# Causal mask of an attention's max pass: added by VectorE in the instruction that takes the maximum, in place of mask matmuls on TensorE

## The chip, the cores and the metric

The kernel runs on one core of a Trainium2 chip. The metric is the time on the device for one execution, in microseconds (us); lower is better. The engines are TensorE (PE in the rows, its weight loads PEld), VectorE (DVE), ScalarE (ACT), GpSimd (POOL) and SyncE (SP), which here only issues DMAs (SPq in the rows).

## The reference, cut to what matters

Two layers, each a mixer and a feed-forward with modulation, over x of 16 batches, 512 tokens, 256 channels. The change touches the mixer of the second layer, a causal attention with 16 heads of 16 channels:

```python
q, k, v = (x @ w_qkv).reshape(B, T, 3, H, HD) ...          # B 16, T 512, H 16, HD 16
scores = einsum('bhqd,bhkd->bhqk', q, k) * SCALE
scores = where(causal, scores, -inf)                        # key after query: never
scores = scores + head_scales * q_proj[..., :, None] * k_proj[..., None, :]
attn = softmax(scores, axis=-1)
out = einsum('bhqk,bhkd->bhqd', attn, v) ... @ w_out
```

The added rank-one term is folded into the q weights, so that one product gives the scores. Softmax subtracts the maximum of each row (each query) over the keys that it may see.

## The kernel before, in words

Ahead of the attention are the first layer and the modulation; behind it are a router and experts. All of these are left as they are. The attention takes 16 batches (NB) one after the other, and in each 16 heads.

**Two passes over the scores.** q and k are written as three bf16 parts each, stored to `qk_parts` in DRAM and loaded again into `q_stack` and `k_stack`, 96 rows of partitions per head (`sp_store`, `sp_load`). The *max pass* computes scores with queries on the partitions (`pe_max`), and VectorE takes the maximum of each row (`dve_max`) into `top`. TensorE turns `top`, VectorE splits it into three bf16 parts (`dve_neg_max`), and SyncE copies these into three more rows of `q_stack` (`sp_row`). The *second pass* computes the scores again, with keys on the partitions and the maximum subtracted by the product itself (`pe_scores`), ScalarE takes the exponential (`act_exp`), and TensorE multiplies it with the values, four heads at a time (`pe_pv`).

**Tiles and banks of the max pass.** A head has four query tiles of 128 rows. Tile qt sees (qt + 1) x 128 keys, so the widths are 512, 384, 128 and 256. They come as three *fills* of a PSUM bank: tile 3; tiles 2 and 0 side by side; tile 1. Two banks are used in turn, fill n (three per head) in bank MAX0 + n % 2. TensorE may write fill n when VectorE has read fill n - 2 (semaphore `mxr`), and VectorE may read it when TensorE's last matmul of the fill is done (`mxp`).

**The mask before.** The last 128 columns of each tile hold the diagonal block. Behind each score matmul, a second one of ident_b with mask_q (128 x 128, bf16, zero or -3.0e38 where key > query) adds the mask to those columns (L1194). The second pass does the same with mask_k (L1212).

**Order of the work.** Each engine's list is written out by hand, one function per engine and batch (`pe_batch`, `dve_batch`, `act_batch`, `sp_batch`), and goes in order. In TensorE's list, at head h and fill f of batch i, the second pass of head h comes first and then the max pass of head h + 7 (AHEAD), which from h = 9 on is a head of batch i + 1. Seven heads of the max pass run ahead of the first batch. Other work stands between the heads: the values at h = 0, the turning of the normed x at 1, the q and k projections of the next batch at 3 and 4, the turning of `top` at 1, 5, 9 and 13, the products with the values at the third fill of 0, 4, 8 and 12, and the output projection of the batch before at 7 and 8. SyncE's list in a batch is: row copy of group 1, stores of q and k parts of the next batch, row copy 2, loads of the next batch's groups 0 and 1 (a group is four heads), row copy 3, load 2, row copy 0 of the next batch, load 3.

The lines of the profile that matter: L1192 score matmul of the max pass, L1194 its mask matmul, L1210 and L1212 the same of the second pass, L1414 the maximum, L1430 to L1437 `dve_neg_max`, L1457 rest of q and k parts, L1544 the exponential, L1638 the third q and k parts on GpSimd, L1659 the stores, L1671 the loads, L1677 the row copies. L2047 and L1469 are VectorE instructions elsewhere that the prediction compares with.

Of the kernel before, what the change touches and what calls it, by code (L numbers as in the profile page):

```python
# [27 lines left out]
P = 128  # L28
# [993 lines left out]
         (1, (0, 3), slice(0, 3)), (1, (3, 5), slice(0, 2)), (1, (5, 6), slice(0, 1)))  # L1022
N_STORES = 2 * 3 * 2
STACK = len(Q_PARTS) * HD


def attention_weights(nc, t, ps, mem, wq, wk, wv, wo, ident_b, mask_q, mask_k):


    with ExitStack() as ctx:  # L1030
        def sb(name, shape, dt=F32):
            return ctx.enter_context(nc.sbuf_tensor("aw_" + name, shape, dt))

        def sem(name):
            return ctx.enter_context(nc.semaphore("aw_" + name))

        f_qT, f_q = sb("qT", [P, DK, D]), sb("q", [P, DK, D])
        f_k, f_v, f_o = sb("k", [P, DK, D]), sb("v", [P, DK, D]), sb("o", [P, DK, D])
        dirs, sdirs, scales = sb("dirs", [HEADS, D]), sb("sdirs", [HEADS, D]), sb("scales", [HEADS, 1])
        form = sb("form", [P, DK, D])  # L1040
        masks = sb("masks", [P, 2, P])
        small, big, fold, prod, hi, lo, const = (sem(n) for n in ("small", "big", "fold", "prod", "hi", "lo", "const"))
        block = ctx.enter_context(nc.Block())

        @block.sync
        def _(sp):
            sp.dma_start(dirs[:, :], t["head_dirs"]).then_inc(small, 16)
            sp.dma_start(scales[:, :], t["head_scales"]).then_inc(small, 16)
            sp.dma_start(f_qT[:, :, :], t["wqT"].rearrange("(k p) n -> p k n", p=P)).then_inc(small, 16)
            for n, f in enumerate((f_k, f_v)):  # L1050
                sp.dma_start(f[:, :, :], t["w_qkv"][:, (n + 1) * D:(n + 2) * D].rearrange(
                    "(k p) n -> p k n", p=P)).then_inc(big, 16)
            sp.dma_start(f_o[:, :, :], t["w_out1"].rearrange("(k p) n -> p k n", p=P)).then_inc(big, 16)
            sp.dma_start(masks[:, :, :], t["masks"].rearrange("n p m -> p n m")).then_inc(big, 16)

        @block.vector
        def _(dve):
            dve.wait_ge(small, 48)
            dve.tensor_scalar(sdirs[:, :], dirs[:, :], scales[:, 0:1], None, ALU.mult).then_inc(fold, 1)
            dve.wait_ge(prod, 1)  # L1060
            dve.tensor_copy(form[:, :, :], ps[:, 0, :].rearrange("p (k n) -> p k n", k=DK)).then_inc(fold, 1)
            dve.wait_ge(fold, 2)
            for m in range(DK):
                d = form[:, m, m * P:(m + 1) * P]
                dve.scalar_tensor_tensor(d, mem["ident"][:, :], ATT_SCALE, d, ALU.mult, ALU.add).then_inc(fold, 1)
            dve.wait_ge(prod, 2)
            dve.tensor_copy(f_q[:, :, :], ps[:, 1, :].rearrange("p (k n) -> p k n", k=DK)).then_inc(fold, 1)
            dve.wait_ge(big, 64)
            dve.tensor_copy(ident_b[:, :], mem["ident"][:, :]).then_inc(const, 1)
            dve.tensor_copy(mask_q[:, :], masks[:, 0, :]).then_inc(const, 1)  # L1070
            dve.tensor_copy(mask_k[:, :], masks[:, 1, :]).then_inc(const, 1)
            for n, (f, w) in enumerate(((f_q, wq), (f_k, wk), (f_v, wv), (f_o, wo))):
                dve.wait_ge(hi, n + 1)
                dve.tensor_tensor(w[1][:, :, :], f[:, :, :], w[0][:, :, :].bitcast(F32), ALU.subtract).then_inc(lo, 1)
            dve.wait_ge(lo, 4)
            dve.wait_ge(const, 3)

        @block.scalar
        def _(act):
            for n, (f, w) in enumerate(((f_q, wq), (f_k, wk), (f_v, wv), (f_o, wo))):  # L1080
                if n == 0:
                    act.wait_ge(fold, 5)
                if n == 1:
                    act.wait_ge(big, 64)
                act.activation(w[0][:, :, :], f[:, :, :], ACT.Copy).then_inc(hi, 1)

        @block.tensor
        def _(pe):
            pe.wait_ge(fold, 1)
            for m in range(DK):  # L1090
                last = pe.matmul(ps[:, 0, m * D:(m + 1) * D], dirs[:, m * P:(m + 1) * P], sdirs[:, :],
                                 start=True, stop=True)
            last.then_inc(prod, 1)
            pe.wait_ge(fold, 4)
            for m in range(DK):
                for k in range(DK):
                    last = pe.matmul(ps[:, 1, m * D:(m + 1) * D], f_qT[:, k, m * P:(m + 1) * P], form[:, k, :],
                                     start=(k == 0), stop=(k == DK - 1))
            last.then_inc(prod, 1)


def attention_stage(nc, t, ps, mem):
# [7 lines left out]
    with ExitStack() as ctx:  # L1110
        def sb(name, shape, dt=F32):
            return ctx.enter_context(nc.sbuf_tensor("at_" + name, shape, dt))
# [5 lines left out]
            return Signal(ctx, nc, "at_" + name, per, before)  # L1118

        wq, wk, wv, wo = (pair(n, [P, DK, D]) for n in ("wq", "wk", "wv", "wo"))  # L1120
        ident_b, mask_q, mask_k = (sb(n, [P, P], BF16) for n in ("ident_b", "mask_q", "mask_k"))
        attention_weights(nc, t, ps, mem, wq, wk, wv, wo, ident_b, mask_q, mask_k)

        parts_dram = nc.dram_tensor("qk_parts", (2, 3, HD, HEADS, T), BF16, kind="Internal").ap()
        q_stack = sb("q_stack", [P, HEADS, T], BF16)
# [53 lines left out]
        def pe_max(pe, b, h, f):  # L1179

            if h % GROUP == 0 and f == 0:
                pe.wait_ge(*loaded[h // GROUP](b, loaded[0].per))
            n = 3 * h + f

            if n >= 2:
                pe.wait_ge(*mxr(b, 4 * ((n - 2) // 3) + (1, 3, 4)[(n - 2) % 3]))
            elif not (isinstance(b, int) and b == 0):
                pe.wait_ge(*mxr(b - 1, 4 * HEADS - 1 + n))
            for qt, col in MAX_TILES[f]:
                w = (qt + 1) * P  # L1190
                out = bank(MAX0 + n % 2)[:, col:col + w]
                pe.matmul(out, q_stack[0:STACK, h, qt * P:(qt + 1) * P], k_stack[0:STACK, h, 0:w],  # L1192
                          start=True, stop=True)
                last = pe.matmul(bank(MAX0 + n % 2)[:, col + w - P:col + w], ident_b[:, :], mask_q[:, :],  # L1194
                                 start=False, stop=True, skip_group_check=True)
            last.then_inc(mxp.sem, 1)

        def pe_scores(pe, b, h, f, first):
# [209 lines left out]
        def dve_max(dve, b, h, fills=(0, 1, 2)):  # L1408
            for f in fills:
                tiles, n = MAX_TILES[f], 3 * h + f  # L1410
                dve.wait_ge(*mxp(b, n + 1))
                for qt, col in tiles:
                    w = (qt + 1) * P
                    dve.tensor_reduce(top[:, h, qt:qt + 1], bank(MAX0 + n % 2)[:, col:col + w], AX.X,  # L1414
                                      ALU.max).then_inc(mxr.sem, 1)

        def dve_hT_lo(dve, b):
            for f in range(DK):
# [1106 lines left out]
```

## Time and profile before

| | us |
|---|---|
| median of 3 runs | 2944.64 |
| lowest and highest of them | 2942.94 and 2945.9 |
| profiled execution, first to last instruction (its span) | 2939.9 |
| TensorE busy | 2435.4 (83%) |
| VectorE busy | 1607.6 (55%) |
| ScalarE busy | 1290.3 (44%) |

The profile gives no other time of its own execution than the span. Busy time is the union of an engine's instructions; a matmul counts from its start to its modelled end, so two that overlap in the pipeline have more duration than they take of the engine. The mean granted clock of TensorE over the span is 0.915 of full speed.

### The profile page before, as it was taken

The numbers are of one execution on the slowest core, as the hardware profiler recorded it, in microseconds if no ns is written. First come the engines' busy times: TensorE is split into PE (matmuls) and PEld (weight loads), VectorE is DVE, ScalarE is ACT, GpSimd is POOL, SyncE is SP. The second block draws the span as 40 slices with busy tenths as digits, with TensorE's granted clock in tenths as the row PEclk, the third lists the DMA queues.
The fourth block names the chain that finished last, engine by engine and source line by source line (L and its number), as shares of the span: only waits on it lengthen the run. The fifth ranks groups of instructions, "written<-read, shape, count | busy, mean of one in ns | idle before, by whom it ended". The sixth has DMA issues, their size and how long they took to land. (4 is left out here: it accounts for less than half of the span.)

```text
span 2939.9 us, 47404 instructions
## 1 busy us (share of the span) xinstructions
PE 2435.4 (83%) x15620; PEld 1842.1 (63%) x15620; DVE 1607.6 (55%) x3588; ACT 1290.3 (44%) x2196; POOL 495.6 (17%) x405
## 2 busy tenths in 40 slices
PE   4999999999689998467788888888888874379997
PEld 4777777777568886335555555555555573269996
DVE  2444444444345443546566665666666565886664
ACT  1444444444345555424455555555555542014442
POOL 0111011011011113300000000001000021025664
PEclk8999999999989998579999999999999986559999
DMA  4100000000100000123222323222222138025543
GB/s 155 55 0 0 0 0 0 0 0 0 29 0 0 0 0 0 36 69 78 70 68 67 73 67 74 67 65 65 74 72 72 44 119 264 0 90 115 122 90 43
DMA packets 123033, 157.38 MB, mean 54 GB/s; under 512 B 26960, under 2 KB 104160, under 8 KB 122848
## 3 DMA queue, kind: packets, MB, share of 16 engines
q1 hardware_dynamic: 108640, 131.20, 16.4%
q0 software_dynamic: 14336, 25.44, 4.5%
q8 instruction: 34, 0.56, 0.1%
q14 instruction: 23, 0.19, 0.0%
HBM read 96.82 MB, written 58.98 MB: 53 GB/s over the span
## 5 line engine op out<-in xcount | busy, mean ns | idle before, releaser
L1414 DVE TENSOR_REDUCE at_top<-psum 128x1 f32<-128x512 f32 (+3 forms) x1024 | 446.8, 483 | 337.8 <-PE psum L1194 335.5
L1544 ACT ACTIVATE at_probs<-psum 128x512 f32<-128x512 f32 (+1 forms) x768 | 372.1, 530 | 409.4 <-PE psum L1212 407.2
L1192 PE MATMUL psum<-at_k_stack,at_q_stack 96*128 96x512 bf16 (+3 forms) x1024 | 297.9, 317 | 171.3 <-DMA at_k_stack<-qk_parts 119.0
L1210 PE MATMUL psum<-at_q_stack,at_k_stack 99*128 99x512 bf16 (+3 forms) x1024 | 290.4, 310 | 43.5 <-DMA at_q_stack<-at_neg_top 27.9
L1192 PEld LDWEIGHTS psum<-at_k_stack,at_q_stack 96*128 96x128 bf16 x1024 | 103.8, 101 | 274.7 <-DVE at_top L1414 103.0
L1194 PE MATMUL psum<-at_mask_q,at_ident_b 128*128 128x128 bf16 x1024 | 207.8, 228 | 0.0
L1212 PE MATMUL psum<-at_mask_k,at_ident_b 128*128 128x128 bf16 x1024 | 203.7, 225 | 0.0
L1210 PEld LDWEIGHTS psum<-at_q_stack,at_k_stack 99*128 99x128 bf16 x1024 | 103.2, 101 | 137.2 <-issue 60.9
L1228 PE MATMUL psum<-at_probs,at_values 128*32 128x512 f32 (+3 forms) x2048 | 151.8, 437 | 0.9 <-ACT at_probs L1544 0.9
L1638 POOL TENSOR_TENSOR at_q_parts<-at_hT,at_q_parts 128x512 bf16<-128x512 f32 x32 | 36.5, 1163 | 683.6 <-ACT at_q_parts L1580 683.6
L576 POOL TENSOR_TENSOR y<-y,mean 128x512 f32<-128x512 f32 x64 | 82.4, 1316 | 347.9 <-ACT mean L618 347.9
L2233 POOL DMA_INDIRECT out<-ex_result,slot_tokens x64 | 119.6, 1869 | 103.8 <-DVE ex_result L2365 89.1
L614 ACT ACTIVATE y_hi<-y 128x512 fp32r<-128x512 f32 x64 | 40.5, 632 | 164.6 <-DVE y L517 164.6
L2411 ACT ACTIVATE ex_mid<-psum,ex_b_up 128x512 f32<-128x512 f32 x96 | 66.2, 690 | 105.5 <-PE psum L61 103.8
L1228 PEld LDWEIGHTS psum<-at_probs,at_values 128*32 128x32 f32 x2048 | 60.1, 110 | 82.4 <-issue 63.7
L59 PE MATMUL psum<-ex_w_down_hi,ex_mid_hi 128*128 128x256 f32 x384 | 108.8, 283 | 0.3 <-DVE ex_mid_lo L2344 0.3
L61 PE MATMUL psum<-ex_w_down_hi,ex_mid_lo 128*128 128x256 f32 x384 | 107.4, 280 | 0.0
L60 PE MATMUL psum<-ex_w_down_lo,ex_mid_hi 128*128 128x256 f32 x384 | 107.4, 280 | 0.0
L59 PE MATMUL psum<-hT_hi,w_in_hi 128*128 128x512 f32 x256 | 102.2, 399 | 3.4 <-DVE hT_lo L487 3.4
L1212 PEld LDWEIGHTS psum<-at_mask_k,at_ident_b 128*128 128x128 bf16 x1024 | 103.8, 101 | 1.5
L1194 PEld LDWEIGHTS psum<-at_mask_q,at_ident_b 128*128 128x128 bf16 x1024 | 104.5, 102 | 0.0
L59 PE MATMUL psum<-h_hi,w_conv_hi 128*128 128x512 f32 x256 | 102.4, 400 | 0.0
(390 smaller groups left out, 6360.6 us busy)
## 6 DMA issues: line engine op xcount, KB each, us to landing
qk_parts<-at_q_parts SPq DMA_DIRECT2D x96, 128.0 KB
qk_parts<-at_k_parts SPq DMA_DIRECT2D x96, 128.0 KB
at_q_stack<-qk_parts SPq DMA_DIRECT2D x64, 192.0 KB
at_k_stack<-qk_parts SPq DMA_DIRECT2D x64, 192.0 KB
x_residual<-in_x SPq DMA_DIRECT2D x16, 512.0 KB, 8.8
at_q_stack<-qk_parts SPq DMA_DIRECT2D x64, 128.0 KB
at_k_stack<-qk_parts SPq DMA_DIRECT2D x64, 128.0 KB
token_rows<-ro_h_tok SPq DMA_DIRECT2D x16, 512.0 KB, 3.1
```

The lines of the kernel that those rows point to most:

```text
L59: pe.matmul(out, w[0], x[0], start=start, stop=False)
L60: pe.matmul(out, w[0], x[1], start=False, stop=False)
L61: return pe.matmul(out, w[1], x[0], start=False, stop=stop)
L576: pool.tensor_tensor(dev[:, m, :], y[:, m, :], mean[:, :], ALU.subtract).then_inc(dv.sem, 1)
L1192: pe.matmul(out, q_stack[0:STACK, h, qt * P:(qt + 1) * P], k_stack[0:STACK, h, 0:w], start=True, stop=True)
L1194: last = pe.matmul(bank(MAX0 + n % 2)[:, col + w - P:col + w], ident_b[:, :], mask_q[:, :], start=False, stop=True, skip_group_check=True)
L1210: pe.matmul(bank(bk)[:, col:col + w], k_stack[0:STACK + 3, h, kt * P:(kt + 1) * P], q_stack[0:STACK + 3, h, kt * P:T], start=True, stop=True)
L1212: last = pe.matmul(bank(bk)[:, col:col + P], ident_b[:, :], mask_k[:, :], start=False, stop=True, skip_group_check=True)
L1228: last = pe.matmul(bank(PV_BANK)[32 * hh:32 * hh + 32, kt * P:T], values[:, kt, GROUP * g + hh, :], probs[:, slot(GROUP * g + hh), P_COL[k ...
L1414: dve.tensor_reduce(top[:, h, qt:qt + 1], bank(MAX0 + n % 2)[:, col:col + w], AX.X, ALU.max).then_inc(mxr.sem, 1)
L1544: act.activation(probs[:, slot(h), 512 * f:512 * f + w], bank(f)[:, 0:w], ACT.Exp).then_inc(ex.sem, 1)
L2233: pool.indirect_dma_start(out=rows_out, out_offset=bass.IndirectOffsetOnAxis(ap=index[:, e, c * TT + a:c * TT + a + 1], axis=0), in_=resul ...
```

## The change

mask_q is gone, and so is the second matmul of each tile in `pe_max`. A tile `later` of 128 x 512 f32 is made once: zero in columns 0 to 383 by a memset, and the mask of the diagonal block in columns 384 to 511. A query tile of width w takes its last w columns, so that the mask lies on the diagonal block. `dve_max` issues one tensor_tensor_reduce per tile: it adds scores (PSUM) and `later` (SBUF), writes the sum back over the scores in PSUM, and folds it by maximum into `top`. The wait for TensorE sits on a nop of its own ahead of a fill's first tile.

```diff
--- before.py
+++ after.py
@@ -1022,9 +1022,10 @@
          (1, (0, 3), slice(0, 3)), (1, (3, 5), slice(0, 2)), (1, (5, 6), slice(0, 1)))
 N_STORES = 2 * 3 * 2
 STACK = len(Q_PARTS) * HD
-
-
-def attention_weights(nc, t, ps, mem, wq, wk, wv, wo, ident_b, mask_q, mask_k):
+LOWEST = -3.0e38
+
+
+def attention_weights(nc, t, ps, mem, wq, wk, wv, wo, ident_b, mask_k, later):
 
 
     with ExitStack() as ctx:
@@ -1067,13 +1068,14 @@
             dve.tensor_copy(f_q[:, :, :], ps[:, 1, :].rearrange("p (k n) -> p k n", k=DK)).then_inc(fold, 1)
             dve.wait_ge(big, 64)
             dve.tensor_copy(ident_b[:, :], mem["ident"][:, :]).then_inc(const, 1)
-            dve.tensor_copy(mask_q[:, :], masks[:, 0, :]).then_inc(const, 1)
+            dve.tensor_copy(later[:, T - P:T], masks[:, 0, :]).then_inc(const, 1)
+            dve.memset(later[:, 0:T - P], 0.0).then_inc(const, 1)
             dve.tensor_copy(mask_k[:, :], masks[:, 1, :]).then_inc(const, 1)
             for n, (f, w) in enumerate(((f_q, wq), (f_k, wk), (f_v, wv), (f_o, wo))):
                 dve.wait_ge(hi, n + 1)
                 dve.tensor_tensor(w[1][:, :, :], f[:, :, :], w[0][:, :, :].bitcast(F32), ALU.subtract).then_inc(lo, 1)
             dve.wait_ge(lo, 4)
-            dve.wait_ge(const, 3)
+            dve.wait_ge(const, 4)
 
         @block.scalar
         def _(act):
@@ -1118,8 +1120,9 @@
             return Signal(ctx, nc, "at_" + name, per, before)
 
         wq, wk, wv, wo = (pair(n, [P, DK, D]) for n in ("wq", "wk", "wv", "wo"))
-        ident_b, mask_q, mask_k = (sb(n, [P, P], BF16) for n in ("ident_b", "mask_q", "mask_k"))
-        attention_weights(nc, t, ps, mem, wq, wk, wv, wo, ident_b, mask_q, mask_k)
+        ident_b, mask_k = (sb(n, [P, P], BF16) for n in ("ident_b", "mask_k"))
+        later = sb("later", [P, T])
+        attention_weights(nc, t, ps, mem, wq, wk, wv, wo, ident_b, mask_k, later)
 
         parts_dram = nc.dram_tensor("qk_parts", (2, 3, HD, HEADS, T), BF16, kind="Internal").ap()
         q_stack = sb("q_stack", [P, HEADS, T], BF16)
@@ -1189,10 +1192,8 @@
             for qt, col in MAX_TILES[f]:
                 w = (qt + 1) * P
                 out = bank(MAX0 + n % 2)[:, col:col + w]
-                pe.matmul(out, q_stack[0:STACK, h, qt * P:(qt + 1) * P], k_stack[0:STACK, h, 0:w],
-                          start=True, stop=True)
-                last = pe.matmul(bank(MAX0 + n % 2)[:, col + w - P:col + w], ident_b[:, :], mask_q[:, :],
-                                 start=False, stop=True, skip_group_check=True)
+                last = pe.matmul(out, q_stack[0:STACK, h, qt * P:(qt + 1) * P], k_stack[0:STACK, h, 0:w],
+                                 start=True, stop=True)
             last.then_inc(mxp.sem, 1)
 
         def pe_scores(pe, b, h, f, first):
@@ -1411,8 +1412,12 @@
                 dve.wait_ge(*mxp(b, n + 1))
                 for qt, col in tiles:
                     w = (qt + 1) * P
-                    dve.tensor_reduce(top[:, h, qt:qt + 1], bank(MAX0 + n % 2)[:, col:col + w], AX.X,
-                                      ALU.max).then_inc(mxr.sem, 1)
+                    if qt == tiles[0][0]:
+                        dve.nop(nofuse=True)
+                    scores = bank(MAX0 + n % 2)[:, col:col + w]
+                    dve.tensor_tensor_reduce(out=scores, in0=scores, in1=later[:, T - w:T], scale=1.0, scalar=LOWEST,
+                                             op0=ALU.add, op1=ALU.max,
+                                             accum_out=top[:, h, qt:qt + 1]).then_inc(mxr.sem, 1)
 
         def dve_hT_lo(dve, b):
             for f in range(DK):
```

## Rows read from the trace of the kernel before

**Rows 1.** The page's head: the span, and each engine's busy time.

```profile
span 2939.9 us, 47404 instructions
PE 2435.4 (83%) x15620; PEld 1842.1 (63%) x15620; DVE 1607.6 (55%) x3588; ACT 1290.3 (44%) x2196; POOL 495.6 (17%) x405
```

**Rows 2.** The page's groups: line, engine, out<-in, count | busy us, mean ns | idle.

```profile
L1194 PE MATMUL psum<-at_mask_q,at_ident_b 128*128 128x128 bf16 x1024 | 207.8, 228 | 0.0
```

**Rows 3.** Waits, 1265 to 2340 us: total us, times, longest us.

```profile
PEld psum L1192 <- DVE at_top L1414: 103.0, 222, 1.4
PE psum L1192 <- DMA at_k_stack<-qk_parts: 93.4, 15, 6.7
PE psum L1192 <- DVE at_top L1414: 48.0, 74, 1.2
```

**Rows 4.** Timeline, 1720 to 1795 us, GpSimd and SyncE: start us, duration us.

```profile
1720.32 2.28 POOL L1638 TENSOR_TENSOR at_k_parts<-at_hT,at_k_parts 128x512 bf16<-128x512 f32 x2 [4.54 <-ACT at_k_parts L1580]
...
1722.62 3.63 SPq L1659 DMA_DIRECT2D qk_parts<-at_k_parts  x6
1726.37 1.83 SPq L1677 DMA_DIRECT2D at_q_stack<-at_neg_top  x3
1729.32 1.97 SPq L1671 DMA_DIRECT2D at_q_stack<-qk_parts  x3
...
1790.81 3.63 SPq L1659 DMA_DIRECT2D qk_parts<-at_k_parts  x6
```

**Rows 5.** Timeline, 1742 to 1763 us, weight loads of TensorE.

```profile
1742.13 0.10 PEld L1192 LDWEIGHTS psum<-at_k_stack,at_q_stack 96*128 96x128 bf16 x1 [6.57 <-issue]
...
1743.18 0.15 PEld L1192 LDWEIGHTS psum<-at_k_stack,at_q_stack 96*128 96x128 bf16 x1
1743.29 0.15 PEld L1194 LDWEIGHTS psum<-at_mask_q,at_ident_b 128*128 128x128 bf16 x1
...
1751.14 0.10 PEld L1192 LDWEIGHTS psum<-at_k_stack,at_q_stack 96*128 96x128 bf16 x1 [0.38 <-DVE at_top L1414]
```

**Rows 6.** Timeline, 1742 to 1763 us, VectorE.

```profile
1742.89 0.69 DVE L1414 TENSOR_REDUCE at_top<-psum 128x1 f32<-128x512 f32 x1 [6.46 <-PE psum L1194]
1744.17 1.08 DVE L1414 TENSOR_REDUCE at_top<-psum 128x1 f32<-128x384 f32 x3 [0.59 <-PE psum L1194]
...
1747.46 1.67 DVE L1414 TENSOR_REDUCE at_top<-psum 128x1 f32<-128x512 f32 x4
...
1749.74 1.68 DVE L1414 TENSOR_REDUCE at_top<-psum 128x1 f32<-128x512 f32 x4
...
1752.63 1.34 DVE L1414 TENSOR_REDUCE at_top<-psum 128x1 f32<-128x512 f32 x3
1755.05 2.32 DVE L1414 TENSOR_REDUCE at_top<-psum 128x1 f32<-128x256 f32 x5 [1.07 <-PE psum L1194]
1757.28 0.27 DVE L1430 TENSOR_SCALAR at_neg_top<-psum 16x128 bf16<-16x128 f32 x1
```

**Rows 7.** Timeline, 1702 to 1705 us, TensorE and ScalarE.

```profile
1702.78 1.09 PE L1246 MATMUL psum<-ident,at_xn 128*128 128x128 f32 x8
...
1704.18 1.45 ACT L1565 ACTIVATE at_hT<-psum,mod 128x512 f32<-128x512 f32 x2 [1.28 <-PE psum L1246]
...
1704.77 0.22 PE L1194 MATMUL psum<-at_mask_q,at_ident_b 128*128 128x128 bf16 x1
...
1704.94 0.27 PE L1210 MATMUL psum<-at_q_stack,at_k_stack 99*128 99x256 bf16 x1
```

**Rows 8.** Groups of VectorE, shapes kept apart.

```profile
L1414 DVE TENSOR_REDUCE at_top<-psum 128x1 f32<-128x512 f32 x256 | 175.3, 685 | 225.3 <-PE psum L1194 223.0
...
L1469 DVE TENSOR_TENSOR x_residual<-x_residual,psum 128x512 f32 x26 | 17.8, 683 | 0.1
```

**Rows 9.** Timeline, 2464.3 to 2467.6 us, VectorE.

```profile
2464.38 0.74 DVE L2047 TENSOR_SCALAR_CACHE_REDUCE ch_hit<-ch_val,ch_cand 128x512 f32<-128x512 f32 x1
2465.05 0.08 DVE L2047 DVE_READ_ACCUMULATOR ch_hit<-ch_val,ch_cand 128x1 f32 x1
2465.05 0.74 DVE L2047 TENSOR_SCALAR_CACHE_REDUCE ch_hit<-ch_val,ch_cand 128x512 f32<-128x512 f32 x1
```

## The prediction

> **What bounds the kernel now.** I read the busy shares first. TensorE is busy 83% of the span and VectorE 55% [rows 1], which suggests that work taken from TensorE and given to VectorE is a good trade. The groups by line say how much is moved: 1024 mask matmuls of the max pass, busy 207.8 us [rows 2]. But a matmul's busy time holds its pipeline, so it is no price. The waits come next. In the attention TensorE waits 93.4 us, in 15 waits (one a batch), for the DMA that loads k_stack, and 103.0 + 48.0 us for VectorE's maxima [rows 3]. So I read one batch in order of time.
>
> The batches repeat: the k parts are stored at 1722.62 and again at 1790.81, so one takes 68.2 us [rows 4]. In it there is one stretch on which neither engine has a hold: GpSimd's last k part starts at 1720.32, SyncE stores, loads from 1729.32, and TensorE, which ran out of work at 1735.56, goes on at 1742.13 after 6.57 us [rows 4, 5]. From 1722.62 to 1742.13, 19.5 us, the DMA alone decides. TensorE's heads 5 to 8 (of this batch) lie beside it and have those 6.57 us in hand. What sets the period is the rest: from the landing at 1742.13 through heads 9 to 15 and heads 0 to 4 of the next batch to its k projection and store.
>
> In heads 9 to 12 of that rest VectorE has no gap: it waits 0.59 us before 1744.17 and then works without a break to 1753.97, through maxima, normalizing, adding and norm [rows 6]. TensorE waits for it there (0.38 us at 1751.14) [rows 5]. At 1755.05 it has waited 1.07 us, since TensorE was in its product with the values, and then it is continuous again up to neg_max at 1757.28, whose result goes by DMA into q_stack and lets the next batch's scores start [rows 6]. In heads 0 to 4 it is TensorE, or a chain through ScalarE, that is late.
>
> **The change, part by part.**
>
> *Masks gone from TensorE.* At full clock two masks and the matmul between them step from 1704.77 to 1704.94, three steps, so 0.057 us each [rows 7]. Right after the DMA wait, at the lower of the two clock levels, the step is 1743.29 - 1743.18 = 0.11 us [rows 5]. All 1024 together are 1024 x 0.057 = 58 us of TensorE's queue, the most that could be won. Heads 5 to 8 win nothing: their gain lengthens the 6.57 us wait. What counts in one batch, in order:
> - head 9: three masks at 0.11 us before the second fill, less the new wait's entry (below, 0.10): -0.23
> - head 12, first two fills, where TensorE sets the start of its product with the values: 3 x 0.057 = -0.17
> - head 12 third fill and head 13 first fill: -0.11, less one entry 0.10: -0.01
> - head 14 and 15 up to the scores: -0.05
> - heads 0 and 4, bound by TensorE: 8 x 0.057 = -0.46
> - heads 1 to 3: the third fill waits for the first maximum, so most of what the earlier masks free turns into wait; -0.05.
> Sum -0.97 us per batch.
>
> *The new instruction on VectorE.* No row shows it. Nearest are three. A tensor_tensor with one PSUM input takes 683 ns, as the maximum (685) [rows 8], so the second input is free: the stream goes at one column per cycle either way. The instruction that reduces beside its main output, L2047, takes 0.74 us and then shows a second record, an accumulator read of 0.08 us; from one to the next it is 2465.05 - 2464.38 = 0.67 us [rows 9]. Two maxima in a row step by 0.60 us (four, 1280 columns, in 1.67 us including the last one's tail) [rows 6]. The surplus is 0.07 us per tile, and I can't say whether it is the accumulator read or the pointer operand that L2047 has and the new one lacks. Bounds: 0 (the pointer was all of it) and 0.15 us (both, one after the other: 0.07 and 0.08). I take 0.067, since a second instruction must pass the engine. The semaphore then comes with the read's end: at the same time as before within 0.01 us. Writing in place into the bank that it reads is in no row either; as low bound nothing, as high bound a second cycle per column (second rival).
>
> The Trainium skill (Vector Engine (DVE) Microarchitecture Reference, section 5.2) gives some 75 ns per instruction beside one column per cycle, for programs of several steps too; by it the main instruction would cost what the maximum does, and the sum below would be the same.
>
> How many of these tiles lie on the path: three in head 9 (second and third fill), four in head 10 and three in head 11, whose end TensorE waits for at 1751.14, make 10; then head 13's four and the first of head 14; then two in heads 2 and 3, behind hT_lo: 17. 17 x 0.067 = +1.14 us per batch. The other 47 lie in idle time, which is 6.46 us before 1742.89 alone [rows 6]; if that cover were gone they would cost 47 x 0.067 = 3.1 us more per batch.
>
> *The nop that takes the wait.* Behind it stand only the fill's own maxima; all of VectorE's queue (the other maxima, neg_max, hT_lo) waits behind those as before. While VectorE is in arrears the wait is over before the engine is free, and the nop costs nothing. Where it sits idle, the start comes later: ScalarE, which enters hT behind such a nop, starts at 1704.18 though the matmuls ended at 1702.78 + 1.09 = 1703.87, 0.3 us, with register work in it [rows 7]; VectorE starts today at once. Bounds 0 and 0.3, taken 0.10, as no register work follows. It is in the sum above, twice (both in the first part), and in the prologue.
>
> *Prologue and weights.* Seven heads of maxima run ahead of the first batch and nothing covers them: per head 4 x 0.067 + 0.10 - 0.11 = 0.26, together +1.8 us. The memset of 384 columns in the weights adds at most 0.5 us once, taken +0.4. Storing the mask as f32 in place of bf16 changes nothing.
>
> *SyncE.* No DMA is added or moved. The queue's row copy between stores and loads starts at 1726.37, right behind the stores' 1722.62 + 3.63: the queue and not VectorE is what it waited for, so later maxima in head 5 don't delay the loads [rows 4].
>
> **Sum.** Per batch +1.14 - 0.97 = +0.17 us; 15 batches +2.6; with prologue and memset +4.8 us. The span profiled is 2939.9 us [rows 1], 4.7 under the median of the runs, 2944.64, which I take as what lies around it; so span 2944.7, time 2949.4, say 2950 us. What can be told from no change here is 0.2%, 5.9 us: the forecast is no measurable change, on the slow side of it. The mean of it is small because two terms of 14 to 17 us cancel; each 0.01 us of a tile's price is worth 2.6 us.
>
> **Rivals.**
> - *The accumulator read costs nothing, TensorE's gain stays.* A tile costs 0.00 to 0.01, the nop nothing. For it: the read and the next main instruction begin at the same time, 2465.05 [rows 9]. Against: the one behind it loads a pointer first, which may be the cover. Then 17 x 0.01 - 0.97 - 0.2 = -1.0 us per batch, -15 us: 2930 us. Chance 0.25.
> - *VectorE becomes the bound, serial read.* At each tile of heads 9 to 14 the read stands alone behind the main instruction: 0.15 us. It decides from 0.08 us a tile on, where the balance leaves the band of 0.2%. 17 x 0.15 - 0.97 = +1.6 us, x 15 = +24, and the prologue 7 x 0.6 = +4: 2972 us. For it: VectorE has not a gap from 1744.17 to 1753.97 [rows 6]. Chance 0.27.
> - *Half rate.* In-place use of one PSUM bank, or reduction beside two inputs, takes two cycles per column. A fill of 512 would then take 0.53 us more, a mean tile of 320 columns 0.33. On the 17 tiles alone that is 17 x 0.33 x 15 = +84 us; at 64 tiles per batch VectorE would ask 64 x 0.4 = 26 us more per batch, of which waits cover most. Taken 3070 us. No row has VectorE writing PSUM. Chance 0.10.
> The Trainium skill (same page, section 7) says that a scalar_tensor_tensor form with two non-bf16 SBUF sources runs at half rate, as no port is left for the accumulator; here one source is in PSUM, and no run so far shows whether that spares it.
> - *The masks weighed more than their step*, because TensorE's queue was the bound in more heads than I count: 40 of the 58 us, less 17 for VectorE: 2922 us. Against it: the 6.57 us wait and VectorE's gapless stretch. Chance 0.05.
>
> **Numbers.** Forecast 0.33, rivals 0.25, 0.27, 0.10, 0.05. The forecast's own spread (plus or minus 5 us) reaches past the band's upper end at 2950.5 in a good third of its cases. So faster by over 0.2%: 0.28; within: 0.28; slower: 0.44. The range runs from 2927, under the first rival, to 2988, over the serial one; half rate is left out, about one in ten, and a little at the lower end. The likeliest case's own range is 2944 to 2956.
>
> **What would show it.** Right: no L1194; the 512 tile's main instruction near 685 ns, with an accumulator read behind it; four tiles in a row 1.9 us in place of 1.67; the wait for k_stack longer than 93.4 us in sum, as heads 5 to 8 give their masks to it; period 68.4. Wrong: a period under 67.5 (the first rival) or over 69.5 (the serial one), 512 columns at 1.2 us (half rate), or a store-to-load chain that is no longer 19.5 us, in which case my split into covered and uncovered heads fails.

## The result, and the profile after

The changed kernel takes 2958.14 us in the median of 15 runs, the kernel before 2943.92 (15 runs); the ratio is 1.0044, with a 95% interval of 1.0028 to 1.006. So it is slower by 0.44%, some 13 us, where 4.8 were worked out. What no step of the prediction holds is the spread: before, the 15 runs lie between 2941.8 and 2949.3 us, after, between 2939.7 and 2968.1.

Only one of them was profiled, and it is the fastest of the 15: 2939.68 us, with a span of 2937.9. The time of an execution follows the mean granted clock of TensorE in it: 0.912 at 2939.7 us, 0.908 at 2944.1, 0.905 at 2958.1, 0.901 at 2968.1 (correlation over the 15: -0.94). The page of the fastest alone would have said that nothing happened. Here are the groups by line of that execution, which answer to [rows 2, 8]:

```profile
L1418 DVE CUSTOM_DVE_ANT_0 psum<-psum,at_later 128x512 f32<-128x512 f32 x256 | 177.6, 694 | 210.4 <-PE psum L1195 209.1 <-issue 0.4
L1418 DVE CUSTOM_DVE_ANT_0 psum<-psum,at_later 128x384 f32<-128x384 f32 x256 | 151.8, 593 | 6.8 <-PE psum L1195 6.6
L1418 DVE DVE_READ_ACCUMULATOR2_ANT at_top<- 128x1 f32 x1024 | 143.3, 140 | 0.0
```

512 columns take 694 ns where the maximum took 685, so adding and writing back in place in PSUM cost no rate here. There is a second record per tile, the accumulator read, 140 ns and not the 82 of L2047. The waits in the attention, answering to [rows 3]:

```profile
PEld psum L1195 <- DVE at_top L1418: 162.4, 225, 1.8
PE psum L1195 <- DVE at_top L1418: 105.1, 208, 1.6
PE psum L1195 <- DMA at_k_stack<-qk_parts: 95.3, 15, 6.6
```

TensorE waits for VectorE 267.5 us where it was 151.0; the wait for the loads is 95.3 (93.4 before). Head 10 on VectorE, in order of time, answers to [rows 6]:

```profile
1743.79 0.69 DVE L1418 CUSTOM_DVE_ANT_0 psum<-psum,at_later 128x512 f32<-128x512 f32 x1
1744.40 0.14 DVE L1418 DVE_READ_ACCUMULATOR2_ANT at_top<- 128x1 f32 x1
1744.40 0.60 DVE L1418 CUSTOM_DVE_ANT_0 psum<-psum,at_later 128x384 f32<-128x384 f32 x1
1744.91 0.14 DVE L1418 DVE_READ_ACCUMULATOR2_ANT at_top<- 128x1 f32 x1
1744.91 0.33 DVE L1418 CUSTOM_DVE_ANT_0 psum<-psum,at_later 128x128 f32<-128x128 f32 x1
1745.16 0.14 DVE L1418 DVE_READ_ACCUMULATOR2_ANT at_top<- 128x1 f32 x1
1745.16 0.47 DVE L1418 CUSTOM_DVE_ANT_0 psum<-psum,at_later 128x256 f32<-128x256 f32 x1
1745.55 0.14 DVE L1418 DVE_READ_ACCUMULATOR2_ANT at_top<- 128x1 f32 x1
```

The steps are 0.61, 0.51, 0.25 and 0.39: 1.76 us from the first start to the last read's, and 1.90 to its end, where the four maxima took 1.67 from start to end. Read and next main instruction start together. The read's own price shows only behind another of its kind: 384 columns step by 0.51 where the maxima stepped by 0.46, 128 by 0.25 (0.20). And `mxr` fires when the read ends, 1744.40 + 0.14 = 1744.54, while the main instruction ends at 1744.48.

The nop, at a fill for which VectorE had been idle, after:

```profile
1697.82 0.38 PE L1195 MATMUL psum<-at_k_stack,at_q_stack 96*128 96x512 bf16 x1
1698.35 0.70 DVE L1418 CUSTOM_DVE_ANT_0 psum<-psum,at_later 128x512 f32<-128x512 f32 x1 [2.84 <-PE psum L1195]
```

and the same place before:

```profile
1701.36 0.22 PE L1194 MATMUL psum<-at_mask_q,at_ident_b 128*128 128x128 bf16 x1
1701.62 0.69 DVE L1414 TENSOR_REDUCE at_top<-psum 128x1 f32<-128x512 f32 x1 [3.02 <-PE psum L1194]
```

and in the run that adds to the kernel before the nop alone (below, its line numbers):

```profile
1708.53 0.22 PE L1194 MATMUL psum<-at_mask_q,at_ident_b 128*128 128x128 bf16 x1
1708.85 0.69 DVE L1416 TENSOR_REDUCE at_top<-psum 128x1 f32<-128x512 f32 x1 [3.02 <-PE psum L1194]
```

From the matmul's end to VectorE's start it is 1698.35 - 1698.20 = 0.15 us after, 0.04 before and 0.10 with the nop alone (medians over all such starts 147, 37 and 107 ns). So the start comes 0.11 later in the changed kernel; 0.07 of it is the nop, and the other 0.04 comes with the new instruction.

### The profile page after: what moved, and what is told of

It reads as the page before. It is cut to its first block and busy times, and to the rows that moved or that the text cites. A ratio compares the mean times of both kernels' runs of the same rounds, so it can differ in the third digit from the quotient of the medians.

```text
span 2937.9 us, 47149 instructions
## 1 busy us (share of the span) xinstructions
PE 2388.1 (81%) x14596; PEld 1784.0 (61%) x14596; DVE 1647.8 (56%) x4613; ACT 1285.5 (44%) x2196; POOL 497.8 (17%) x405
## 5 line engine op out<-in xcount | busy, mean ns | idle before, releaser
L1418 DVE CUSTOM_DVE_ANT_0 psum<-psum,at_later 128x512 f32<-128x512 f32 (+3 forms) x1024 | 476.1, 518 | 303.6 <-PE psum L1195 301.9
L1195 PE MATMUL psum<-at_k_stack,at_q_stack 96*128 96x512 bf16 (+3 forms) x1024 | 284.9, 321 | 225.6 <-DMA at_k_stack<-qk_parts 120.1
L1211 PE MATMUL psum<-at_q_stack,at_k_stack 99*128 99x512 bf16 (+3 forms) x1024 | 296.7, 316 | 36.7 <-DMA at_q_stack<-at_neg_top 20.8
L1195 PEld LDWEIGHTS psum<-at_k_stack,at_q_stack 96*128 96x128 bf16 x1024 | 93.5, 102 | 317.7 <-DVE at_top L1418 163.5
L1418 DVE DVE_READ_ACCUMULATOR2_ANT at_top<- 128x1 f32 x1024 | 143.3, 140 | 0.0
L2226 POOL DMA_INDIRECT x_residual<-token_rows,slot_tokens x64 | 67.7, 1058 | 201.7 <-issue 201.7
```

Source lines behind the costliest of these rows:

```text
L1195: last = pe.matmul(out, q_stack[0:STACK, h, qt * P:(qt + 1) * P], k_stack[0:STACK, h, 0:w], start=True, stop=True)
L1211: pe.matmul(bank(bk)[:, col:col + w], k_stack[0:STACK + 3, h, kt * P:(kt + 1) * P], q_stack[0:STACK + 3, h, kt * P:T], start=True, stop=True)
L1418: dve.tensor_tensor_reduce(out=scores, in0=scores, in1=later[:, T - w:T], scale=1.0, scalar=LOWEST, op0=ALU.add, op1=ALU.max, accum_out=to ...
L2226: pool.indirect_dma_start(out=tok[u][:, a, :], out_offset=None, in_=rows_dram[:, :], in_offset=bass.IndirectOffsetOnAxis(ap=index[:, e, c ...
```

## The experiments

Ratios are against the kernel before, run on the same chip beside them (median 2943.9 us for the first row, 2945.7 to 2946.4 for the others).

| kernel | ratio, 95% interval | median us |
|---|---|---|
| the change | 1.0044 (1.0028 to 1.006) | 2958.1 |
| the change again | 1.0045 (1.0027 to 1.0064) | 2959.8 |
| masks on TensorE and new instruction | 1.0095 (1.008 to 1.011) | 2972.9 |
| no mask at all, old maximum | 0.9976 (0.9966 to 0.9987) | 2940.0 |
| nop alone | 1.0024 (1.0015 to 1.0032) | 2953.0 |
| the change, columns put back in heads 9 to 15 | 1.0021 (1.0012 to 1.003) | 2953.0 |
| new instruction for two heads of 16 | 0.9976 (0.9967 to 0.9986) | 2938.7 |
| before, wait for the loads filled | 0.9939 (0.9925 to 0.9953) | 2928.4 |
| the change, wait filled | 1.001 (1.0001 to 1.002) | 2949.6 |
| the change, wait filled, columns put back | 0.9987 (0.9978 to 0.9996) | 2942.9 |
| two heads, wait filled | 0.9913 (0.9899 to 0.9926) | 2920.9 |
| two heads, wait filled with 29 | 0.9918 (0.9904 to 0.9931) | 2921.9 |

**The change again.** No edit.

> The changed kernel unaltered, to see a profile of another execution. Its 15 timed runs lay between 2939.7 and 2968.1 us, with the granted clock falling from 0.912 to 0.900 as the time rises; the one profiled was the fastest, and showed 5 stretches of 3.4 us at the lower clock near a batch's end, beside the one stretch of 6.8 us per batch that both kernels have. Theory A (the clock): the added time is these extra stretches; where the profiled run is slower than 2940 us by x, it shows more of them, about one per 2 us of x, and batches without one are 68.2 us as before. Theory B (VectorE's price alone): the number of low stretches stays 5, and all batches are longer by the same amount, up to 1 us.

This time a long execution was profiled, with a span of 2974.4 us. The same stretch of the attention in three executions; behind the busy times stand the granted clock, the DMA share and GB/s. Before:

```profile
1350.00:2300.00 950.00, 783.50 (x6771) 516.06 (x6772) 592.28 (x1526) 489.02 (x972) 76.88 (x69) 0.95 0.29 70
```

after, the short execution:

```profile
1350.00:2300.00 950.00, 746.81 (x5910) 469.26 (x5911) 629.31 (x2418) 486.26 (x974) 77.04 (x69) 0.94 0.28 70
```

after, the long one:

```profile
1350.00:2300.00 950.00, 751.22 (x5740) 462.52 (x5739) 615.11 (x2356) 475.37 (x951) 77.08 (x69) 0.91 0.28 67
```

0.95, 0.94, 0.91. In the long execution one batch, in five stretches, shows where the clock is at its lower level, 1.2 GHz (0.50):

```profile
1472.00:1479.00 7.00, 5.82 (x27) 4.22 (x28) 4.62 (x16) 1.64 (x4) 0.00 (x0) 0.50 0.13 50
1479.00:1486.00 7.00, 6.21 (x62) 3.38 (x60) 6.45 (x27) 3.59 (x7) 0.00 (x0) 0.97 0.18 35
1486.20:1493.00 6.80, 5.12 (x42) 3.22 (x41) 6.00 (x25) 4.22 (x10) 0.00 (x0) 1.00 0.37 75
1493.00:1499.80 6.80, 6.53 (x38) 2.33 (x39) 3.24 (x14) 2.04 (x4) 0.00 (x0) 0.50 0.50 81
1499.80:1506.00 6.20, 5.97 (x61) 4.77 (x54) 2.28 (x11) 3.32 (x7) 0.00 (x0) 1.00 0.12 38
```

The first is the stretch behind the wait for the loads, which the kernel before has too. The fourth, 1493.0 to 1499.8, is new: it begins as head 15 ends and lies over head 0 with its product with the values, where TensorE sets the pace. Before, the same stretch of a batch:

```profile
1687.20:1694.00 6.80, 5.27 (x50) 3.35 (x48) 6.45 (x18) 4.36 (x10) 0.00 (x0) 1.00 0.24 50
1694.00:1700.80 6.80, 6.80 (x72) 4.94 (x72) 2.05 (x5) 2.67 (x5) 0.00 (x0) 1.00 0.49 96
```

What TensorE did before the clock fell at 1493.0, and as it fell, weight loads with a wait for VectorE in the long execution:

```profile
1487.95 0.10 PEld L1195 LDWEIGHTS psum<-at_k_stack,at_q_stack 96*128 96x128 bf16 x1 [0.43 <-DVE at_top L1418]
...
1491.40 0.10 PEld L1195 LDWEIGHTS psum<-at_k_stack,at_q_stack 96*128 96x128 bf16 x1 [1.50 <-DVE at_top L1418]
1492.16 0.10 PEld L1195 LDWEIGHTS psum<-at_k_stack,at_q_stack 96*128 96x128 bf16 x1 [0.54 <-DVE at_top L1418]
1493.52 0.10 PEld L1195 LDWEIGHTS psum<-at_k_stack,at_q_stack 96*128 96x128 bf16 x1 [0.46 <-DVE at_top L1418]
```

That is 2.9 us of waits for VectorE in 6.0 us. At the end of the batch of [rows 5] the kernel before has the same four, and its mask matmuls between:

```profile
1756.35 0.10 PEld L1192 LDWEIGHTS psum<-at_k_stack,at_q_stack 96*128 96x128 bf16 x1 [0.16 <-DVE at_top L1414]
1759.70 0.10 PEld L1192 LDWEIGHTS psum<-at_k_stack,at_q_stack 96*128 96x128 bf16 x1 [1.21 <-DVE at_top L1414]
1760.37 0.10 PEld L1192 LDWEIGHTS psum<-at_k_stack,at_q_stack 96*128 96x128 bf16 x1 [0.38 <-DVE at_top L1414]
1761.60 0.10 PEld L1192 LDWEIGHTS psum<-at_k_stack,at_q_stack 96*128 96x128 bf16 x1 [0.16 <-DVE at_top L1414]
```

Together that is 1.9 us. By the clock's records between 1265 and 2350 us, the long execution has 212 us at the lower level, the short one 123 and the kernel before 106. By the starts of the heads, and over the batches of the 950 us, head 0 takes 8.5 us in the mean, 6.9 before, and the other heads as in the short execution to 0.2 us; the two batches in a row without an extra stretch take 68.2 and 68.0 us. So theory A holds against B: head 0 takes 1.6 us more in the mean, and 8.9 to 9.4 us in eight of these 13 batches. That it comes and goes between executions of one program, by their phase against whatever grants the clock, is my reading and not shown.

**Masks on TensorE, and the new instruction.** VectorE's price alone.

```diff
 # the kernel after against this run, cut
-            dve.tensor_copy(later[:, T - P:T], masks[:, 0, :]).then_inc(const, 1)
-            dve.memset(later[:, 0:T - P], 0.0).then_inc(const, 1)
+            dve.tensor_copy(mask_q[:, :], masks[:, 0, :]).then_inc(const, 1)
+            dve.memset(later[:, :], 0.0).then_inc(const, 1)
 # pe_max: score matmul and mask matmul as before
```

> Mask matmuls kept as in the kernel before, and the new VectorE instruction too, with a tile of zeros to add: VectorE's price alone. Theory B (price): a tile steps by 0.05 us more, a fill that VectorE waits for starts 0.11 us later, so 17 x 0.05 + 3 x 0.11 = 1.2 us per batch, +18 us: 2962 us, in a band as narrow as before (8 us). Theory A (clock): TensorE's work is as dense as before, so the extra low stretches near a batch's end are fewer than in the changed kernel; time between 2944 and 2962, clock 0.910 or more.

Ratio 1.0095, +28 us, the four timed runs within 4.2 us. The profiled one has a clock of 0.94, and of 14 batches behind the first one alone has a stretch at the lower level over its head 0, at 1354 us:

```profile
1350.00:2300.00 950.00, 777.29 (x6653) 508.39 (x6650) 623.24 (x2386) 482.26 (x959) 77.05 (x69) 0.94 0.28 68
```

So with TensorE as dense as before the price is 28 us and steady: theory B's number (18) was a third too small. Per batch it was not (the table behind the experiments has 1.3 us, B 1.2); the rest stands in the profile at a first store of the k parts 2.1 us later, in that one batch, and in work of the first and the last batch that comes once. Some of it is the clock's too, which has 123 us at the lower level and not 106. A's claim that the extra stretches need the thinner TensorE holds but for one.

**No mask, old maximum.** TensorE's gain alone. The mask of the max pass is left out, so the result is not right; the scores are scaled by 0.05 besides, so that nothing overflows (not shown in the cut).

```diff
-                last = pe.matmul(bank(MAX0 + n % 2)[:, col + w - P:col + w], ident_b[:, :], mask_q[:, :],
-                                 start=False, stop=True, skip_group_check=True)
```

> Leaves out the mask in the max pass altogether (and scales the scores by 0.05, so that nothing overflows): TensorE's gain alone, with the old maximum on VectorE. Theory B (sum of terms as predicted): -0.97 us and no nop, so about -1.0 to -1.2 us per batch, -15 to -18 us: 2927 us. Theory A (clock): thinner work on TensorE brings extra low stretches by itself, and what each batch gains is given back: 2935 to 2955 us, spread over more than 15 us from run to run. Theory C (lock): the batch's wait for the loads and the low stretch that follows it keep a fixed distance, so that a batch that is shorter has more of its work at the low clock; the period stays 68.2 to 68.3 us whatever is saved, and the time within 3 us of before.

Ratio 0.9976, -7 us by the ratio, where B has 15 to 18 and C has 0 to 3. Extra low stretches are there without any new instruction, 154 us at the lower level in all, and the clock is 0.93:

```profile
1350.00:2300.00 950.00, 754.39 (x5926) 470.75 (x5924) 589.64 (x1537) 487.40 (x978) 76.95 (x69) 0.93 0.29 70
```

Its head 0 takes 7.6 us in the mean, and it takes either 6.6 or, under a low stretch, 8.1 to 9.6. Batches of the first kind take 66.8 us from store to store, 1.5 less than before, and the five of the second kind 69.7, 1.4 more. Over half of the gain is given back to the clock: A's mechanism, though its spread of over 15 us did not come (9.5). C falls.

**The nop alone.**

```diff
+                    if qt == tiles[0][0]:
+                        dve.nop(nofuse=True)
                     dve.tensor_reduce(top[:, h, qt:qt + 1], bank(MAX0 + n % 2)[:, col:col + w], AX.X,
```

> The kernel before with the nop alone ahead of each fill's first maximum. Theory B: 0.11 us at each fill for which VectorE sits idle on the path, some 3 per batch: +5 us. Theory A and C: within 0.2% of before (6 us).

Ratio 1.0024, +7 us, over each theory. At the 0.07 us measured that would be some six or seven places a batch on the path, and not two; which they are is not shown. It is a quarter of VectorE's 28 us.

**Columns put back in heads 9 to 15.** The changed kernel; in `pe_scores`:

```diff
+                if 9 <= h:
+                    pe.matmul(bank(bk)[:, col:col + P], k_stack[0:STACK + 3, h, kt * P:(kt + 1) * P],
+                              q_stack[0:STACK + 3, h, kt * P:(kt + 1) * P], start=True, stop=True)
                 pe.matmul(bank(bk)[:, col:col + w], k_stack[0:STACK + 3, h, kt * P:(kt + 1) * P],
```

> The changed kernel, with as many columns as the masks had put back on TensorE in heads 9 to 15, where VectorE does not wait for them: each score matmul of the second pass is preceded by one of 128 columns into the same place, which it overwrites (28 a batch, 0.057 us each). Theory A (the clock): the second low stretch of a batch, which in the slow execution lay over head 0 (8.5 us in place of 6.9), comes from TensorE's thinner work in heads 9 to 15; here it goes, the period is 68.1 to 69 us, the time 2943 to 2955, with a spread from run to run as narrow as before's, and the granted clock 0.911 or more. Theory B (all is VectorE's price): nothing is won and 28 x 0.057 = 1.6 us per batch are added where TensorE is late: 2960 to 2983.

Ratio 1.0021 (up to 1.003), against 1.0045 (from 1.0027) for the change again. Work without use, added to the engine that was to be relieved, makes the kernel 5 to 7 us faster, and the runs lie within 8 us in place of 28. The two intervals just touch; the pair with the fill, below, shows the same 7 us with intervals apart. The median of the granted clock is 0.913, against 0.904 in the changed kernel again. In the profiled execution three stretches over a head 0 are left. This decides for A. The 7 us are what is left of the clock's gain when the columns' own time is paid: batches with no stretch over head 0 take 68.5 us, against 67.9 and 68.2 in the changed kernel.

**The new instruction for two heads only.** `pe_max` and `dve_max` take the new way for heads 7 and 11, whose max pass stands beside heads 0 and 4, and the old way for the rest. Cut to the choice on TensorE:

```diff
+BY_VECTOR = (7, 11)
+                if h not in BY_VECTOR:
+                    last = pe.matmul(bank(MAX0 + n % 2)[:, col + w - P:col + w], ident_b[:, :], mask_q[:, :],
+                                     start=False, stop=True, skip_group_check=True)
```

> The new instruction without mask matmuls only for the two heads whose max pass falls to heads 0 and 4 of a batch, where TensorE sets the pace and VectorE is idle; masks and the old maximum for the other 14. By the terms measured: 8 masks x 0.057 = -0.46 us per batch, VectorE's price hidden, one or two later starts of 0.11 us of which TensorE waits for none: -7 us, 2939. Theory A: heads 9 to 15 are as dense as before, so no extra low stretches, spread narrow. Theory C (the period is tied to the low stretch behind the wait for the loads): what is saved in front of that stretch puts more work under it, and half or more of the 7 us is given back: 2942 to 2946.

2938.73 us, ratio 0.9976: the 7 us of the sum, to within the interval. Nothing is given back, so theory C falls here too.

**The wait for the loads filled.** In the kernel before, and in the changed one; the wait for the loads moves from ahead of the wait for the bank to behind the added matmuls, which run in the 15 batches that have a next one:

```diff
+            if h == 0 and f == 0 and ahead:
+                for _ in range(24):
+                    pe.matmul(bank(MAX0 + n % 2), q_stack[0:STACK, 9, 0:P], k_stack[0:STACK, 9, :], start=True, stop=True)
+            if h % GROUP == 0 and f == 0:
+                pe.wait_ge(*loaded[h // GROUP](b, loaded[0].per))
```

> The kernel before, with 24 matmuls of 512 columns without use (into a free bank of the max pass, before the wait for the loads), so that TensorE is not idle in the 6.6 us in which it waits for k_stack. If the low stretch of 6.8 us in each batch comes from that wait, it goes, and the work behind the wait runs at full clock: heads 9 and 10 shorten by 1 to 3 us per batch, 15 to 45 us in all: 2900 to 2930. If 24 x 0.21 = 5.1 us are more than the wait leaves, or the clock falls all the same: 2945 or more.

> The changed kernel with the same 24 matmuls. Theory A: the low stretch behind the wait goes; whether the one over head 0 goes too depends on heads 9 to 15, which are as thin as in the changed kernel, so the difference to the kernel before with the fill is +5 to +25 us, with a wide spread. Theory C: without the tie to the low stretch the terms predicted add up plainly: +0.2 to +0.5 us per batch, +3 to +8 us against the kernel before with the fill.

The kernel before with the fill: 2928.4 us, ratio 0.9939. The timeline of TensorE shows the 24 matmuls and the first one behind the loads:

```profile
1730.11 5.34 PE L1189 MATMUL psum<-at_k_stack,at_q_stack 96*128 96x512 bf16 x24
1736.52 0.39 PE L1195 MATMUL psum<-at_k_stack,at_q_stack 96*128 96x512 bf16 x1 [1.07 <-DMA at_k_stack<-qk_parts]
1736.75 0.22 PE L1197 MATMUL psum<-at_mask_q,at_ident_b 128*128 128x128 bf16 x1
1736.81 0.33 PE L1213 MATMUL psum<-at_q_stack,at_k_stack 99*128 99x384 bf16 x1
...
1741.72 0.28 PE L1195 MATMUL psum<-at_k_stack,at_q_stack 96*128 96x256 bf16 x1 [1.07 <-DVE at_top L1417]
```

The wait left is 1.07 us, and the mask matmul behind it steps by 0.06 us, where it was 0.11 [rows 5]. No stretch at the lower level is left in the 950 us:

```profile
1350.00:2300.00 950.00, 846.92 (x7255) 536.01 (x7256) 602.16 (x1552) 496.08 (x988) 76.92 (x69) 1.00 0.29 71
```

So the low stretch of each batch did come from that wait. It costs 18 us and not the 45 of the upper estimate: at full clock TensorE soon runs into VectorE again (1.07 us at 1741.72).

The changed kernel with the fill is 21 us slower than the kernel before with the fill (1.001 against 0.9939), and most of its low stretches lie over head 0 (in 10 of 14 batches):

```profile
1350.00:2300.00 950.00, 806.08 (x6197) 482.74 (x6195) 626.69 (x2409) 483.07 (x970) 77.09 (x69) 0.97 0.28 70
```

With the large low stretch gone from both, the difference between them is not smaller but larger. The plain sum (C's +3 to +8) is wrong, A's +5 to +25 right.

**Both, and the best version.**

> The changed kernel with both: the 24 matmuls in the wait for the loads, and the 128 columns back in each second-pass matmul of heads 9 to 15. With the fill alone it was 2949.6, 21 us over the kernel before with the fill, and still had 15 low stretches over the heads at a batch's start. Theory A (these come from the thin heads 9 to 15): they go, period 67.6 to 67.9 us, head 0 back to 6.9, time 2936 to 2942; what is then left over 2928 is VectorE's price less TensorE's gain at full clock. Theory B: the added columns cost and nothing is won: 2950 or more.

> The new instruction for the two heads of a batch where TensorE sets the pace (ratio 0.9976 by itself), and the 24 matmuls in the wait for the loads (0.9939 by itself). If the two are independent, which theory A says as no low stretch is left in the steady batches, the ratio is 0.9915, 2921 us; theory C (what shortens heads 0 to 4 was partly given back under the low stretch, which is gone here) says a little more, 2918.

> As the mixed kernel with the fill, but 29 matmuls in place of 24, 6.2 of the 6.6 us of wait. If the wait left over behind the 24 costs clock, 1 to 5 us less; if the fill now ends behind the loads in some batches, since the wait varies from batch to batch by some tenths of a us, 0 to 5 us more.

The changed kernel with fill and columns put back: 0.9987, again 7 us better than without the columns (1.001), clock 0.99, five stretches left in the 950 us. It misses A's upper bound by 1 us:

```profile
1350.00:2300.00 950.00, 816.35 (x6606) 501.47 (x6605) 629.62 (x2425) 485.56 (x975) 76.92 (x69) 0.99 0.29 70
```

Two heads and the fill: 2920.92 us, ratio 0.9913 where the product of the two alone is 0.9915. It beats both kernels by 0.9% and 1.3%. 29 matmuls in place of 24 change nothing that can be told (0.9918).

**Batches with and without a low stretch over head 0.** From the profiled execution of each kernel: us from one store of the k parts to the next, in the mean, and in brackets how many of the 14 batches behind the first. A batch counts as one with a stretch when the clock's records show the lower level at any time in its head 0.

| kernel | without | with |
|---|---|---|
| before | 68.36 (14) | none |
| the change, short execution | 67.91 (9) | 68.56 (5) |
| the change, long execution | 68.22 (2) | 70.75 (12) |
| masks on TensorE and new instruction | 69.66 (13) | 71.61 (1) |
| no mask at all, old maximum | 66.83 (9) | 69.73 (5) |
| the change, columns put back | 68.53 (11) | 70.28 (3) |
| before, wait filled | 67.16 (14) | none |
| the change, wait filled | 67.08 (4) | 69.08 (10) |
| the change, wait filled, columns put back | 67.60 (10) | 69.71 (4) |

Against the kernel before, and without such a stretch, VectorE's price is 1.3 us a batch and TensorE's gain 1.5, and the changed kernel is no slower than the kernel before, with the fill or without. What it loses, it loses in the batches of the right column. These are one execution of each, and some groups are small.

## Why the prediction was right or wrong

The range held the time, and slower was the likelier of the three by the chances given; the forecast, no measurable change at 2950 us, missed it by 8 us, and the time lies 2 us outside the likeliest case's own range. That the wide range held it is in part luck: its upper end came from a dearer VectorE, and what the time went to is the clock, which the prediction takes as unchanged. By its steps:

- *What bounds the batch.* Right. The stretch from store to landing is the same 19.5 us after (stores at 1719.10, first weights behind the wait at 1738.56), and the wait for the loads grew, 95.3 us for 93.4, as the masks gone from heads 5 to 8 should make it.
- *A tile's price on VectorE*, taken 0.067, bounds 0 and 0.15. Measured 0.01 for a tile behind another instruction and 0.05 behind one of its kind, so 0.04 in the mean; but the signal comes 0.06 later, with the read's end, where 0.01 was taken. In the heads where TensorE waits for a fill's first maximum this second term should count, and the prediction had none of it; no run has it alone.
- *Half rate.* Wrong: 694 ns for 512 columns. The loss that the Trainium skill notes for the form with two non-bf16 SBUF sources (Vector Engine (DVE) Microarchitecture Reference, section 7) does not show here with one source in PSUM. Its 1.04 ns per column and some 75 ns per instruction (section 5.2) give 0.61 us for 512 columns, an estimate, and the trace agrees: the step is 0.61; for 384 and 128 they give 0.48 and 0.21, and the steps behind one of its kind are 0.51 and 0.25.
- *The nop*, 0.10 per start from idle: 0.07 alone, 0.11 together with the new instruction. The number of places was too small: 7 us, where two a batch and the prologue made 3.7.
- *VectorE in sum.* The sum had 17 x 0.067 x 15 = 17 us, 3 for the nop in the batches and 2.2 once, 22 in all. Measured, with TensorE's work kept: 28. Per batch the terms were right, 17 x 0.067 and two starts making 1.34 us, where batches without a low stretch over head 0 show 1.3; too small is what stands outside the steady batches.
- *TensorE's gain.* The sum had 1.17 us per batch (0.97 and the two starts taken off in it), 18 us. Of it the part in heads 0 and 4 was right, 7 of 7 us by the mixed kernel. The whole is there too where the clock stays, 1.5 us a batch in the kernel without a mask; but that kernel as a whole gains 7 us and not 15 to 18.
- *The step that failed* is one that the prediction does not write down: it prices every mask at the step of its place and takes the granted clock of each stretch as it was, so a change of the clock stands in the sum at nothing. The masks in heads 9 to 15 did two things, and the prediction saw one: they took TensorE's time, and they kept TensorE busy between waits for VectorE. Without them the clock falls in many batches just before or in head 0, and such a batch is 0.7 us longer in the short execution and 2.5 in the long one.
- *The sum.* It had +0.17 us per batch. Batches without a low stretch over head 0 have -0.45 and -0.14, and with the wait filled -0.08, so the cancelling of the two terms came about as worked out, each a little off. The 0.44%, 13 us, go with the clock. Of them 7 us come back with the columns put back, in both pairs of runs; the columns cost 0.3 to 0.6 us a batch themselves, so the clock's part is some 12 to 16 us, an estimate, which leaves next to nothing for the rest. That the kernel with columns put back stands at +6 us, near the 4.8 of the sum, is chance: it pays for the columns.
- *What would show it.* The period was named as the test, 68.4 us. It is 68.2 in the short execution and 70.2 in the long one, so one profile could confirm nothing. The test that was missing is the granted clock per stretch.

What stays open: why one execution of the same program has an extra low stretch in 5 batches and another in most. The columns put back do not remove all of them and cost time themselves, so their 7 us are a lower bound of the clock's part. That heads 9 to 15 are the place where TensorE's work must stay rests on the waits of one batch and on runs that put columns back there and nowhere else.

## What to carry to other kernels

Work on TensorE that stands between its waits for another engine is not only cost: before it is moved away, ask what the clock does where TensorE then idles, and which work lies under the stretch that follows. Move an instruction's work only where the receiving engine has idle time and the giving one sets the pace: here two heads of 16, -7 us, where all 16 cost 13. Where the spread of the changed kernel is wider than that of the one before, profile it more than once and set the granted clock beside the time before reading anything else.

## What the runs showed of the hardware

- Adding useless matmuls made two kernels faster: 24 x 512 columns a batch in a wait of 6.6 us, -18 us (0.61%); 28 x 128 columns a batch among waits of 0.4 to 1.5 us, -7 us.
- VectorE reads and writes the same PSUM bank in one instruction as fast as it reads alone: 694 ns for 512 columns, against 685.
- The accumulator read of this instruction takes 140 ns, that of the built-in one 82. It starts together with the next main instruction, and costs it 0.05 us only if that is of the same kind (a tensor_tensor of 512 columns behind it steps by 0.60 us, as before).
- A wait on a nop in place of the instruction: 0.07 us from idle (107 ns from the matmul's end, against 37). In arrears it costs nothing: a maximum behind a tensor_tensor of 512 columns starts 0.61 us after it with and without the nop.
